# One-hots of a graph kernel: rows built chunk by chunk, keys compared in one operation against 16-bit values

## The reference

```python
h = jnp.maximum(_layernorm(x, axis=-1), 0.0)
xr = jnp.einsum('nd,rde->rne', h, W_rel)              # 3 relations
msg = xr[edge_type, edge_src] + b_rel[edge_type]
agg = jax.ops.segment_sum(msg, edge_dst, num_segments=N_NODES)
xs = jnp.einsum('nd,tde->tne', h, W_self)             # 3 node types
x = x + jax.nn.relu(xs[node_type, arange] + b_self[node_type] + agg)
# layer 1: layernorm, relu, attention over the same edges (8 heads of 64), projection, residual
```

## Time and profile before

| what | value |
|---|---|
| median of 3 runs | 315.65 us (315.42 to 315.82) |
| span of the profiled execution | 314.1 us |
| rest around the span (median less span) | 1.5 us |
| TensorE busy | 290.3 us, 92% |
| VectorE busy | 199.0 us, 63% |
| one-hots of keys (L838), 120 instructions | 37.0 us |
| one-hots of rows (L845), 20 instructions | 19.0 us |
| matmuls of the windows (L1107), 120 | 33.2 us |

### The profile page before, as it was taken

How to read it: one execution, slowest core, us unless ns; L and a number is a source line. 1 busy time by engine, 2 the same in 40 slices (tenths; PEclk the granted TensorE clock), 3 DMA queues, 4 the chain that set the end, 5 groups by cost and what they waited for, 6 DMA issues and landing times.

```text
span 314.1 us, 5396 instructions
## 1 busy us (share of the span) xinstructions
PE 290.3 (92%) x1966; PEld 226.7 (72%) x1966; DVE 199.0 (63%) x481; ACT 143.6 (46%) x282; POOL 66.8 (21%) x98
## 2 busy tenths in 40 slices
PE   2848799999999999999899999999799999999995
PEld 1512254554677788678787889999689998999984
DVE  6899977997143344334356952884887858676742
ACT  1151344442425422424334441677867666665731
POOL 7042004210383234630001510320000102020202
PEclk9999999999999999999999999999999999999999
DMA  5765980110162400032600000000000000000001
GB/s 184 262 239 200 374 329 34 44 60 34 39 206 97 136 3 3 2 134 57 213 0 0 2 0 3 0 0 3 0 2 0 37 2 0 37 0 35 3 33 32
DMA packets 10970, 22.29 MB, mean 71 GB/s; under 512 B 950, under 2 KB 966, under 8 KB 10938
## 3 DMA queue, kind: packets, MB, share of 16 engines
q1 hardware_dynamic: 8772, 16.80, 15.5%
q0 software_dynamic: 800, 2.62, 2.2%
q10 hardware_dynamic: 1366, 2.45, 2.1%
HBM read 15.60 MB, written 6.26 MB: 70 GB/s over the span
## 4 chain that ended last, share of the span: by engine, by line
PE 79%; DVE 12%; ACT 3%; DMA 2%; issue 2%; DVEq 0%
PE banks L1264 14%; PE banks L1209 9%; PE banks L1250 9%; PE banks L1154 8%; PE banks L1352 7%; PE banks L1336 7%; PE banks L1107 6%; PE banks L1325 6%; PE banks L1374 4%; DVE key_hot L838 3%; DVE row_hot L845 2%; DMA raw<-in_L_gnn_W_qkv_dram 2%; PE banks L1239 1%; PE banks L1196 1%; PE banks L1364 1%
## 5 line engine op out<-in xcount | busy, mean ns | idle before, releaser
L1107 PE MATMUL banks<-key_hot,row_hot 128*128 128x480 f16 x120 | 33.2, 427 | 8.8 <-DVE key_hot L838 8.7
L1021 DVE CUSTOM_DVE_ANT_0 s_sb<-banks,mask_add 128x640 f32<-128x640 f32 x40 | 32.4, 821 | 12.8 <-PE banks L1325 12.6
L678 ACT ACTIVATE p_sb<-s_sb,neg_max 128x640 f32<-128x640 f32 x40 | 32.9, 825 | 12.4 <-DVE neg_max L1021 12.1
L838 DVE TENSOR_SCALAR key_hot<-iota,picked 128x480 f16<-128x480 f16 x120 | 37.0, 375 | 0.0
L1209 PE MATMUL banks<-adjT,h 128*128 128x320 f16 x240 | 33.1, 299 | 0.4 <-DVE zT_even L897 0.4
L1107 PEld LDWEIGHTS banks<-key_hot,row_hot 128*128 128x128 f16 x120 | 12.8, 107 | 26.7 <-DVE key_hot L838 9.6
L1209 PEld LDWEIGHTS banks<-adjT,h 128*128 128x128 f16 x240 | 23.3, 98 | 9.8 <-DVE zT_even L897 0.7
L1336 PE MATMUL banks<-ident,p_sb 128*128 128x128 f32 x200 | 29.8, 275 | 0.4 <-ACT pT L685 0.2
L1264 PE MATMUL banks<-w_hl,zT_even 128*128 128x512 f32 x120 | 29.3, 394 | 0.0
L1325 PE MATMUL banks<-k_hi,q_st 128*128 128x320 f32 x80 | 26.5, 340 | 2.0 <-DVE neg_max L1021 2.0
L1250 PE MATMUL banks<-h2T,wqkvT 128*128 128x320 f32 (+1 forms) x192 | 28.1, 308 | 0.0
(11 more groups left out here) (179 smaller groups left out, 468.6 us busy)
## 6 DMA issues: line engine op xcount, KB each, us to landing
w_self<-in_L_gnn_W_self_dram SPq DMA_DIRECT2D x3, 1024.0 KB, 9.3
raw<-in_L_gnn_W_rel_dram SPq DMA_DIRECT2D x3, 1024.0 KB, 15.6
raw<-in_L_gnn_W_qkv_dram SPq DMA_DIRECT2D x3, 1024.0 KB, 5.4
sorted_rows<-zero_rows ACTq DMA_DIRECT2D x1, 1792.0 KB, 10.5
self_rows<-hs SPq DMA_DIRECT2D x7, 256.0 KB, 2.0
hs<-sorted_rows SPq DMA_DIRECT2D x1, 1280.0 KB, 7.1
xs<-in_x_dram SPq DMA_DIRECT2D x1, 1024.0 KB
raw<-in_L_gnn_W_ff_dram SPq DMA_DIRECT2D x1, 1024.0 KB
```

Of the source, the lines that this page charges most:

```text
L678: nc.scalar.activation(p_sb[:, n % NPR, :], s_sb[:, n % NS, :], ACT.Exp, scale=-1.0, bias=neg_max[:, it, h:h + 1], accum_out=denom[:, it, ...
L838: return nc.vector.tensor_scalar(to_key, iota[:], float(KEYS * w), key, ALU.add, ALU.is_equal)
L1021: nc.vector.tensor_tensor_reduce(s_sb[:, n % NS, :].rearrange("p (a j) -> p a j", a=2), banks[:, c:c + 2, 0:HALF], mask_add[:, it, :].rear ...
L1107: mm(banks[:, w % 2, 0:KEYS], row_hot[:, w % 2, k, :], key_hot[:, w % 2, k, :], start=(k == 0), stop=True, skip_group_check=True).then_inc ...
```

## The change

It does three things.

1. The rows of a chunk are compared by an instruction of their own (128 columns, the row as a scalar for each partition in 16 bits) ahead of the chunk's keys, in place of one instruction for all six chunks of a window.
2. The keys are stored less 480w, in 16 bits (`picked_key`), so that one comparison without an addition makes the one-hot.
3. `picked` goes. Two instructions read the bank of PSUM directly: one writes `picked_row` (plus 1), one writes `picked_key` (less `span_key`, a new constant of GpSimd). GpSimd has two smaller fills and one iota in place of one fill, and the counts of `s_fill` that others wait for rise by 2.

```diff
-        picked = place("picked", o_r4 + 55808, [P, 2, NW * G], F32)
-        picked_row = place("picked_row", o_r4 + 61504, [P, NW * G], F16)
+        picked_key = place("picked_key", o_r4 + 55808, [P, NW, G], F16)
+        picked_row = place("picked_row", o_r4 + 56064, [P, NW * G], F16)
+        span_key = place("span_key", o_r4 + 56320, [P, NW], F32)
...
-        FILLS = 25
+        FILLS = 27
...
-            nc.gpsimd.memset(picked[:], 0.0).then_inc(s_fill, 1)
+            nc.gpsimd.memset(picked_key[:], 0.0).then_inc(s_fill, 1)
+            nc.gpsimd.memset(picked_row[:], 0.0).then_inc(s_fill, 1)
+            nc.gpsimd.iota(span_key[:], [[KEYS, NW]], base=0, channel_multiplier=0,
+                           allow_small_or_imprecise_dtypes=True).then_inc(s_fill, 1)
...
-            nc.vector.tensor_copy(picked[0:EL], banks[0:EL, 4, 0:2 * NW * G].rearrange("p (k c) -> p k c", k=2)
-                                  ).then_inc(s_keys, 1)
+            dve.wait_ge(s_fill, 13)
+            nc.vector.tensor_scalar(picked_row[0:EL], banks[0:EL, 4, 0:NW * G], 1.0, None, ALU.add)
+            nc.vector.tensor_tensor(picked_key[0:EL],
+                                    banks[0:EL, 4, NW * G:2 * NW * G].rearrange("p (w k) -> p w k", w=NW),
+                                    span_key[0:EL].unsqueeze(2).broadcast_to([EL, NW, G]), ALU.subtract
+                                    ).then_inc(s_keys, 1)
...
-                nc.vector.tensor_tensor(row_hot[:, par], iota[:, 0:P].unsqueeze(1).broadcast_to([P, G, P]),
-                                        picked_row[:, w * G:(w + 1) * G].unsqueeze(2).broadcast_to([P, G, P]),
-                                        ALU.is_equal)
                 for k in range(G):
                     n = w * G + k
-                    key_one_hot(key_hot[:, par, k, :], picked[:, 1, n:n + 1], w).then_inc(s_hot, 1)
+                    nc.vector.tensor_scalar(row_hot[:, par, k, :], iota[:, 0:P], picked_row[:, n:n + 1], None,
+                                            ALU.is_equal)
+                    nc.vector.tensor_scalar(key_hot[:, par, k, :], iota[:], picked_key[:, w, k:k + 1], None,
+                                            ALU.is_equal).then_inc(s_hot, 1)
...
             dve.wait_ge(s_keys, PICKED)
-            dve.wait_ge(s_fill, 11)
-            chain(nc.vector.tensor_scalar(picked_row[:], picked[:, 0, :], 1.0, None, ALU.add))
             node_types()
             hot_group(0)
```

More of the change, by code:

```diff
@@ L442, in _ @@
                            allow_small_or_imprecise_dtypes=True).then_inc(s_fill, 1)
-            pool.wait_ge(s_fill, 17)
+            pool.wait_ge(s_fill, 19)
             nc.gpsimd.memset(full[:, 0:1], -1.0).then_inc(s_fill, 1)
@@ L449, in _ @@
             nc.gpsimd.memset(eps_c[:], EPS).then_inc(s_fill, 1)
-            pool.wait_ge(s_fill, 20)
+            pool.wait_ge(s_fill, 22)
             for r in range(R):
@@ L834, in one_hots @@
                 nc.vector.tensor_scalar(to_row, iota[:, 0:P], -1.0, row, ALU.add, ALU.is_equal)
-                return key_one_hot(to_key, key, w)
-            def key_one_hot(to_key, key, w):
                 return nc.vector.tensor_scalar(to_key, iota[:], float(KEYS * w), key, ALU.add, ALU.is_equal)
```

## The result

| | kernel before | changed kernel |
|---|---|---|
| median | 315.66 us (20 runs, 315.2 to 317.19) | 316.72 us (20 runs, 315.98 to 320.6) |
| span of the profiled execution | 314.1 us | 314.3 us |
| busy: TensorE, VectorE | 290.3, 199.0 us | 291.6, 200.6 us |

The ratio is 1.0043, with a 95% interval of 1.0026 to 1.006: the change makes the kernel slower, by 1.06 us in the medians. The forecast was 316.1 us, range 314.0 to 317.6, with "same" (within 0.2%) as the likeliest answer. The time lies in the range; the likeliest answer did not come.

The account below looks back on a forecast made before the run. VectorE's groups of windows 0 to 8 were taken to bound the start, TensorE the rest. Groups +1.0, picks -0.20, waits -0.16 and -0.30, GpSimd +0.10 gave +0.45 us: 316.1 us, range 314.0 to 317.6.

Parts of the forecast that it names:

- the prices of the instructions: VectorE's one-hots: a row instruction for one chunk takes 0.164 us, a key stays at 0.255 us.
- picks -0.20: VectorE's two picks ahead of group 0: 0.50 us in place of 0.70, so -0.20 us.
- rival D: VectorE's new row instruction runs at one column a step: +6.2 us, 322 us; chance 0.03.
- rival A: VectorE's row instruction has only the small fixed part, 0.10 us: -1.9 us, 313.8 us; chance 0.09.
- B: VectorE reads the 16-bit scalar for nothing, in rows and keys: -4.2 us, 311.4 us; chance 0.05.
- 0.3 us more of fills there is hidden: GpSimd's early fills: 0.3 us more of them costs nothing, hidden by the 4.4 us until the picks at 8.40.
- the wait at group 5, -0.30: VectorE's wait for TensorE's window 3 before group 5 is used up by longer groups: -0.30 us.
- GpSimd's +0.10: While GpSimd issues scatters, one or two more VectorE instructions are held: +0.10 us, bounds 0 and +0.3.
- the wait at the places: VectorE's 0.16 us wait for TensorE at 15.53, by the places table, goes: -0.16 us.
- cover a shift either way of 4 us: Sorted rows issued at 27.61 land by 34.7, before their use at 39.5, so shifts of 4 us cost nothing.
- Rival C: TensorE's one-at-a-time pace in windows 6 to 8 drops it to 1.2 GHz, costing 2.5 us: 318.6 us; chance 0.10.
- E: The groups are not the limit; only the two waits and the picks move: 315.2 to 315.7 us; chance 0.05.

Follow-up runs that it names:

- early_only: Changed kernel with the rows chunk by chunk in windows 0 to 8 only, later windows in one instruction: 316.9 us, ratio 1.0039.
- rows_only: Kernel before with the row one-hots chunk by chunk; picks, keys and fills as they were: 318.27 us, ratio 1.007.
- trace of 316.02 us: First profiled execution of the changed kernel, one of its two fastest runs: span 314.3 us.
- again: Changed kernel once more with no edit, for a second profile: 317.5 us, ratio 1.0048 against the kernel before.
- picks_keys: Changed kernel with the rows of a window in one instruction as before, new picks and keys kept: 315.14 us, ratio 0.9983.
- early_zeros: Changed kernel with ScalarE's transfer of zeros issued ahead of its wait for x: 316.29 us, ratio 1.0018.
- rows_one_op_2_to_4: Changed kernel with the rows of windows 2, 3 and 4 in one instruction each: 315.5 us, ratio 0.9997.
- rows_two_input: Changed kernel with each chunk's row compared by a two-input instruction of 128 columns: 332.7 us.
- small_gap: Changed kernel with an extra two-input instruction of 2 columns at the head of groups 2, 3 and 4: 328.65 us.

## Why the prediction was right or wrong

**Right: the prices of the instructions.** Row 0.1625 (forecast 0.164), key 0.254 with the scalar in 16 bits and one operation (0.255), picks -0.20. Groups 5 to 8 together went from 9.82 to 10.24 us, 0.105 each (forecast 0.11). The fixed part of 0.13 us was taken from the keys, 0.255 less 0.125 for their columns, and it decides this change: six instructions pay 0.78 us of it, where one paid 0.07. With one column a step (rival D) a row would have taken 0.27 us, with only the small fixed part (rival A) 0.10. Rivals A, B and D are out. That the scalar makes the fixed part longer still rests on L804 and L809 alone. The scalar in 16 bits costs what the one in 32 bits did, 0.254 us a key and 0.255. The Trainium skill says in "DVE: scalar operands, raw-bit mode, write accounting and state across instructions" (section 1) that a bf16 scale costs the same as one in fp32. The trace agrees for the 16-bit scalar here.

**Right: what bounds the kernel.** Only the groups up to window 8 count (early_only, against the changed kernel).

**Wrong: "0.3 us more of fills there is hidden".** The forecast looked at who waits for the fills' semaphore, and nobody does. But VectorE's L722 and L724 (L718 and L720 before), at 3 us, stand until GpSimd is through with its fill of `edge_keys`. VectorE and GpSimd of the changed kernel:

```profile
3.04 1.16 DVE L722 TENSOR_SCALAR tiles_i<-edges_i 80x125 int32<-80x125 int32 x1
3.17 1.09 DVE L724 TENSOR_SCALAR tiles_i<-edges_i 80x125 int32<-80x125 int32 x1
4.30 0.28 DVE L725 SCALAR_TENSOR_TENSOR edges_f<-tiles_i,edges_i 80x125 f32<-80x125 int32 x1
```
```profile
3.38 0.53 POOL L434 IOTA iota<- 128x480 f16 x1
3.87 0.25 POOL L436 MEMSET edge_keys<- 128x192 f32 x1
```

and VectorE with the old fills, in rows_only:

```profile
3.02 1.02 DVE L718 TENSOR_SCALAR tiles_i<-edges_i 80x125 int32<-80x125 int32 x1
3.15 0.95 DVE L720 TENSOR_SCALAR tiles_i<-edges_i 80x125 int32<-80x125 int32 x1
4.14 0.28 DVE L721 SCALAR_TENSOR_TENSOR edges_f<-tiles_i,edges_i 80x125 f32<-80x125 int32 x1
```

Two instructions of 125 columns take over 1 us together, and what follows starts at 4.30 in place of 4.14. The iota stands at 3.38 in place of 3.22: the two fills more ahead of it are 0.16 us, and VectorE is 0.16 later. The first instruction on the edges starts at 2.57 to 2.78 in different traces, and that made no difference. TensorE's first matmul behind it starts at 6.46 to 6.48 in all 12 traces with the new fills, and at 6.33 in the two with the old ones (before and rows_only). So the fills cost 0.15 us on the chain. Put behind L440 they would probably cost nothing; that wasn't tried.

**Wrong: the wait at group 5, -0.30, and GpSimd's +0.10.** The two go together. Of groups 2 to 4 the forecast said that they would grow by 0.11 each and be held by GpSimd once or twice. But before, scatters had lengthened the keys of groups 2 and 3 to 2.57 and 2.55 us a group; now VectorE is not held at all, and they are 2.50 (the step had no term for that gain). VectorE gets to group 5 at 28.79, not 29.3, and TensorE's window 3 is done only at 29. The wait of 0.23 stays. It covers what the two groups saved. In sum, by starts of the row instructions, group 0 to the end of group 8 went from 9.24 to 39.12, 29.88 us, to 9.20 to 39.26, 30.06.

The ledger to the first product in the trace of 316.02 us: +0.15 fills, -0.19 picks, -0.17 from group 0 to the start of group 1 (+0.10 for the group, the rest is the wait and what stood behind it), -0.10 to group 4, +0.03 to group 5, +0.42 to the end of group 8: +0.14. The forecast had +0.45. Alone, this trace would have said that the change is cheaper than forecast. Of the terms, rows, picks and the wait at the places came out; the wait at group 5 (-0.30 forecast), GpSimd (+0.10) and the fills (0) did not, and their errors partly cancel.

**Wrong, and it decided the result: the sorted rows "cover a shift either way of 4 us".** The step took the issue of `hs` as a time that moves with VectorE by tenths. It is not: the scatters ahead of it are issued by GpSimd beside VectorE's one-hots, and in some executions one is held for 8.1 to 8.3 us (again, rows_only, early_only). Then `hs` goes out at 36.65 to 36.90. The cover was also computed for the wrong transfer. `hs` comes in two, and TensorE's first transposes need only the first, which the profile of before lists beside the 1280 KB of the earlier trace rows:

```profile
hs<-sorted_rows SPq DMA_DIRECT2D x1, 512.0 KB, 3.7
```

It landed at 31.35, so the cover was 39.47 - 31.35 = 8.1 us and not 39.5 - 34.7 = 4.8. That is why issues of `hs` 6.0 and 6.5 us later than before (picks_keys, early_zeros) cost no wait. The held scatters make it 9.0 to 9.3 us later. That uses up even the 8.1 us, and TensorE waits 0.87 to 1.38 us. On top, in two of these three profiles, TensorE ran the first products partly at 1.2 GHz, 1.6 to 1.7 us more. That makes 317.5 us without the drop, and 318.7 and 319.1 with it; the median of 316.72 lies between these and the undisturbed 316. Bringing the scatters forward removes the tail (early_zeros), and so does taking the short instructions away beside them (rows_one_op_2_to_4). That the slower executions of the changed kernel are those with late rows is shown by the profiled ones; the others have no profile.

So of the +1.06 us some 0.6 is the pure change (early_zeros, 0.2 to 0.9 by its interval) and the rest late rows. Of the 0.6 only 0.14 to 0.18 can be seen at the first product; the rest is not placed, and two traces can differ by 0.35 us in parts behind it that the change does not touch. The sign of the forecast's sum was right, and the pure change is near its +0.45. But that the time of 316.72 us lies in the stated range is in part luck: the late rows were in none of its terms, and with the rows part alone (rows_only) the median of 318.27 us is past the upper bound. The forecast had GpSimd hold VectorE, since that was what the trace of before shows in the earlier trace rows, and it did not ask what VectorE does to GpSimd once no long instruction stands between the keys. The Trainium skill has the mechanism in "SBUF — State Buffer" (section "Who interferes with whom"): a VectorE instruction in a mode that uses both ports shares a port pair with GpSimd, whoever starts first keeps it for the whole instruction, and the other waits; descriptors of GpSimd's transfers are written through it (that part the page calls inferred). The traces agree in kind, in both directions (at 3.04 us and at 21). They go beyond it in size: by the end of one instruction a hold would last 0.33 us, and these lasted 4.5 to 12.7 us, over 20 and more instructions. And by that section an instruction with two inputs does not hold up such a transfer; with one between every two keys (rows_two_input) they were held the longest. The keys around it are still of the kind that can, so this does not contradict the page.

**Rival C** had its effect right in some executions, but its trigger is not borne out: with the pace of windows 6 to 8 the level held in the trace of 316.02 us, and it fell without that pace in picks_keys. **E** is refuted by groups 5 to 8.

**Open.** Why a scatter gets through in one execution (1.0 to 1.4 us) and not in the next is not settled. small_gap ran once in 315.78 us and five times in some 329; the same program, the same instructions. One lead is when the first scatter starts, 0.86 us after the zeros have landed. Among the traces with the changed one-hots and the zeros where they were, it got through when it started at 20.49 (the first trace) and was held when it started at 20.71 to 20.89 (again, rows_only, early_only); group 2 starts at 21.29 to 21.33. These are four traces, and later scatters do not follow it: one at 21.97 got through, one at 21.73 (early_zeros) did not. The holds of again, rows_only and early_only all ended at 28.98 to 29.02, beside the first key of group 5, where VectorE had no gap; those of picks_keys ended once a group, near the row instruction. The fine order in time of the two engines' starts may decide it; no run here separates that.

## What to carry to other kernels

An operation cut into pieces pays its fixed part for each: take it from instructions of the same form, because those with a scalar for each partition had 0.13 us here and others 0.05 to 0.07. If GpSimd issues transfers, or fills constants, beside a dense run of short VectorE instructions, ask in both directions who holds whom, and compute the cover of what hangs on it for the transfer that is needed first and for the held case, not for the one in the profile. If the runs of a kernel spread more after a change than before, one profile of it is not enough: profile it again until a slow one is among them.

## What the runs showed of the hardware that was not expected

- An issue of an indirect transfer by GpSimd takes 0.96 to 1.4 us when it gets through, about 2.1 to 2.5 us when it is held for one group (picks_keys), and 4.5 to 12.7 us when it is held beside VectorE's short one-hots. In the changed kernel VectorE shows nothing of it: its instructions keep their 0.1625 and 0.254 us.
- The reverse at 3 us: two VectorE instructions of 125 columns stand about 1 us until GpSimd's fills up to `edge_keys` are done, and two more fills ahead of it cost their full 0.16 us.
- Three more instructions of 0.07 us each beside the scatters cost 12 us in five of six executions (small_gap): the time jumps between executions and does not grow with the work.
- A wait of 1.3 to 1.4 us behind a stretch in which TensorE was half busy was followed by part of its products at 1.2 GHz (5.32 and 5.39 us for eight, in place of 3.70); one of 0.87 us behind the same stretch was not (3.70). In picks_keys the level fell at window 8 with gaps of 0.83 to 0.90 us in front of it, so the length of one wait does not decide it.
- The late issue did not change how long `hs` takes by much: its 512 KB landed 3.76 us after the issue of the second trace and 3.74 in before, its 1280 KB 7.7 us after it and 7.1 in before.
